# Turning patches with plain identity products, and products that nobody reads in TensorE's waits

## The reference, cut to what matters

```python
x  # (4, 3, 224, 224)
patches = x.reshape(b, c, hp, P, wp, P)              # P = 8, so 28 x 28 patches of 8 x 8 x 3 = 192 features
patches = jnp.transpose(patches, (0, 2, 4, 3, 5, 1)).reshape(b, hp * wp, P * P * c)
tokens = layernorm(patches, ln1_g, ln1_b)
tokens = tokens @ W1 + b1                            # 192 -> 64
tokens = layernorm(tokens, ln2_g, ln2_b)
h1 = layernorm(tokens @ Wp1 + bp1, lnp_g, lnp_b)     # the same rows three times over
return jax.nn.silu(h1) @ Wp2 + bp2
```

## Time and profile before

| what | value |
|---|---|
| median of the timed runs | 605.25 us (603.64 to 606.86) |
| span of the profiled execution | 604.2 us |
| TensorE busy | 561.1 us, 93% of the span |
| VectorE busy | 376.7 us, 62% |
| ScalarE busy | 337.7 us, 56% |
| chain that ended last, TensorE's share | 90% |

### The profile page before, as it was taken

One profiled execution on the slowest core, in us unless ns is written; L12 is line 12 of the kernel. 1 busy time (PEld: TensorE's weight loads), 2 busy tenths in 40 slices (PEclk: granted clock), 3 DMA queues, 4 the chain that ended last, 5 costly groups with the idle time before them and its releaser, 6 DMA issues.

```text
span 604.2 us, 10259 instructions
## 1 busy us (share of the span) xinstructions
PE 561.1 (93%) x3082; PEld 327.0 (54%) x3082; DVE 376.7 (62%) x899; ACT 337.7 (56%) x734; POOL 81.6 (14%) x97
## 2 busy tenths in 40 slices
PE   0699899998999999999999999999999999998993
PEld 0454334443465666666665675675675676544341
DVE  3844654324787676676676676676676677354471
ACT  0464858666674664664564564564564564657331
POOL 0000000000998001001001001001001001120000
PEclk9999799999989999999999999999999999999998
DMA  7500000001623223323223323223323320000015
GB/s 173 230 0 1 1 0 2 0 14 33 157 84 86 73 65 93 79 63 97 72 61 98 73 60 97 75 59 98 76 58 98 76 58 19 2 1 1 1 33 128
DMA packets 21986, 37.65 MB, mean 62 GB/s; under 512 B 5560, under 2 KB 15224, under 8 KB 21704
## 3 DMA queue, kind: packets, MB, share of 16 engines
q1 hardware_dynamic: 21606, 36.82, 23.6%
q10 hardware_dynamic: 354, 0.50, 0.3%
HBM read 6.07 MB, written 2.41 MB: 14 GB/s over the span
## 4 chain that ended last, share of the span: by engine, by line
PE 90%; DVE 3%; ACT 3%; DMA 2%; issue 1%; SPq 0%; DVEq 0%
PE P L775 86%; DMA X<-x 2%; PE P L791 2%; ACT L528 1%; DVE mx L1590 1%; PE P L1089 1%; PE P L1283 1%; DVE bst L1367 1%; SPq L399 0%; ACT PT L655 0%; ACT g L701 0%; PE P L917 0%; DVE xhat L1439 0%; PE P L1072 0%; DVE xn L1380 0%
## 5 line engine op out<-in xcount | busy, mean ns | idle before, releaser
L1590 DVE TENSOR_REDUCE mx<-P 112x1 f32<-112x392 f32 x448 | 218.8, 557 | 93.7 <-PE P L775 89.5
L655 ACT ACTIVATE PT<-P 112x392 f32<-112x392 f32 x448 | 188.5, 495 | 27.3 <-PE P L775 26.0
L775 PE MATMUL P<-Ks,Qs 96*112 96x392 f32 x448 | 166.8, 377 | 0.7 <-ACT XV L623 0.6
L775 PE MATMUL P<-Qs,Ks 98*112 98x392 f32 x448 | 154.0, 349 | 0.8 <-ACT PT L655 0.7
L775 PE MATMUL P<-PT,XVs 112*64 112x392 f32 x896 | 154.7, 496 | 0.0
L775 PEld LDWEIGHTS P<-PT,XVs 112*64 112x64 f32 x896 | 61.4, 137 | 80.0 <-issue 74.2
L775 PEld LDWEIGHTS P<-Ks,Qs 96*112 96x112 f32 x448 | 78.2, 177 | 44.0 <-issue 18.9
L663 ACT ACTIVATE CT<-P 128x392 f32<-128x392 f32 x32 | 15.9, 498 | 128.0 <-PE P L775 128.0
L775 PEld LDWEIGHTS P<-Qs,Ks 98*112 98x112 f32 x448 | 79.1, 178 | 4.8 <-ACT PT L655 2.6
L753 POOL TENSOR_TENSOR OUT<-OUT,part 120x448 f32<-120x448 f32 x27 | 31.1, 1151 | 264.7 <-DVE part L1617 264.7
L775 PE MATMUL P<-VBs,CT 128*112 128x130 f32 (+1 forms) x320 | 40.0, 261 | 0.0
(11 more groups left out here) (197 smaller groups left out, 477.7 us busy)
## 6 DMA issues: line engine op xcount, KB each, us to landing
Qs<-QKH SPq DMA_DIRECT2D x64, 98.0 KB, 2.2
Ks<-QKH SPq DMA_DIRECT2D x64, 98.0 KB, 2.1
XVs<-XV SPq DMA_DIRECT2D x32, 196.0 KB, 2.5
Qs<-QKL SPq DMA_DIRECT2D x32, 98.0 KB, 2.1
Ks<-QKL SPq DMA_DIRECT2D x32, 98.0 KB, 2.1
X<-x SPq DMA_DIRECT2D x4, 588.0 KB
wa<-table_a SPq DMA_DIRECT2D x1, 2207.5 KB, 8.5
VBs<-VB SPq DMA_DIRECT2D x32, 65.0 KB, 2.2
```

Source lines behind the costliest of these rows:

```text
L655: nc.scalar.activation(PT[:, u, c * HALF:(c + 1) * HALF], P[0:T, SCORE_BANK + half_in_loop(s, u, c) % RING, 0:HALF], ACT.Exp, scale=float( ...
L775: return nc.tensor.matmul(dst, lhsT, rhs, start=start, stop=stop, **more)
L1590: nc.vector.tensor_reduce(mx[:, s % 2, c, t:t + 1], bank(n)[0:T, :], AX.X, ALU.max)\
```

## The change

`turn` uses a plain product with the identity (patches as weights, the first 112 columns of the identity as the moving operand) in place of the transpose instruction. A new helper `busy(n, times)` multiplies the identity by the first 389 columns of the table into PSUM bank n; nobody reads that bank before other products overwrite it. It is called in five places of TensorE's stream: three products as soon as the pixels are in and ahead of turn(0); two after project(6); one in the first norm's `weights(2)`; one each in the second norm's `folded(1)` and `folded(2)`; two after the second norm's spread, ahead of the products with wp2c.

```diff
@@ -788,9 +788,13 @@
                 pe.wait_ge(xn_ready, g + 1)
                 for q in range(4):
                     for k in range(2):
-                        last = nc.tensor.transpose(P[0:KF, 2 * p + k, q * T:(q + 1) * T], xn[:, p, q, k * KF:(k + 1) * KF],
-                                                   A("ident", T)[:, 0:T])
+                        last = mm(P[0:KF, 2 * p + k, q * T:(q + 1) * T], xn[:, p, q, k * KF:(k + 1) * KF], A("ident", T)[:, 0:T])
                 last.then_inc(turned, 1)
+
+            def busy(n, times):
+
+                for _ in range(times):
+                    mm(P[:, n, 0:EARLY_A], A("ident"), wa[:, 0:EARLY_A])
 
             def project(g, p):
                 pe.wait_ge(xT_ready, 2 * g + 2)
@@ -800,6 +804,8 @@
                                   k == 0, k == 1)
                 last.then_inc(patch_full, 1)
 
+            pe.wait_ge(pixels_in, 16 * B)
+            busy(6, 3)
             turn(0, 0)
             pe.wait_ge(w1_ready, 1)
 
@@ -810,6 +816,7 @@
                 project(2 * i + 1, 1)
             repeat(pe, 0, 3, {}, two)
             project(6, 0)
+            busy(6, 2)
 
 
             def norm(S, source=None, count=None, meanwhile=None):
@@ -847,12 +854,15 @@
                 elif b == 2:
                     pe.wait_ge(bias_in, 1)
                     mm(P[:, 0, 0:1], wp1c[:, :], col("ln2_b")).then_inc(bias_full, 1)
+                    busy(6, 1)
 
             def folded(b):
                 if b == 0:
                     for h in range(2):
                         last = mm(P[h * D:(h + 1) * D, 5, 0:HEADS * D], A("fold", D), A("vo", D))
                     last.then_inc(vo_full, 1)
+                elif b < B - 1:
+                    busy(7, 1)
 
             pe.wait_ge(means_set, 1)
             norm(TOK2, meanwhile=weights)
@@ -862,6 +872,7 @@
                 mm(bank(b), wp1g[:, :], xhat[:, b, :]).then_inc(main_full, 1)
             pe.wait_ge(woy_ready, 1)
             norm(POOL3, meanwhile=folded)
+            busy(7, 2)
             for b in range(B):
                 pe.wait_ge(silu_ready, b + 1)
                 mm(bank(b), wp2c[:, :], act[:, b, :]).then_inc(centred, 1)
```

## The result

The changed kernel took 596.45 us (median of four executions, 596.15 to 598.7) beside 605.49 us for the kernel before (603.64 to 606.86); the ratio is 0.986 with an interval of 0.984 to 0.989. The profiled execution has a span of 594.3 us and a time of its own of 596.15, so 1.85 us lie outside the span. A span and the time of the same execution are thus two things, also for the kernel before, where the span of 604.2 was taken as the time.

What follows compares the result with a forecast made beforehand. TensorE at half clock was taken to bound the patch stage; gains of 2.4 (patches), 1.8 (first norm), 2.65 (wp1g) and 0.75 (second norm) sum to 7.6, span 604.2 to 596.6, plus 1.05 gives 597.6 us, range 595 to 600.

Steps and rivals of the forecast that it cites:

- the likeliest case: Whole kernel: the forecast of 597.6 us holds, with its own range of 595 to 600; chance 0.72.
- the largest term: Patch stage: TensorE at full clock shortens the groups, put at -2.4 us after a 0.3 charge.
- The turn at full clock: Patch stage: 16 plain-product instructions take 1.67 us at full clock, as long as the transposes were.
- the projection: Patch stage: each group's projection on TensorE goes from 1.69 to about 0.95 us at full clock.
- The third rival: Patch turns: a plain product costs four transposes, so a turn takes 2.99 us, the kernel 605.1; chance 0.02.
- The group: Patch stage: one turn-and-projection group goes from 3.35 to 2.8 us, five groups gaining 2.7.
- the loop over ScalarE and VectorE: Patch stage: turn, ScalarE, VectorE, then next-but-one turn take 5.65 us per two groups, setting 2.8 a group.
- the 0.3 I charged for a late rise: Patch stage: 0.3 us taken off the gain because the clock rises only between 19.4 and 21.9 us.
- First norm: First norm: variances -0.65, `weights` no longer delaying the spread -0.4, spread -0.75; -1.8 us together.
- wp1g to the second norm's spread: Products with wp1g to the second norm's variances: 7.09 us becomes 4.4 at full clock, a gain of 2.65.
- the second spread: Second norm: the spread at full clock gains 0.75 us, its fillers fitting into existing waits.
- the first rival: Clock lost again where no filler is, likeliest the third norm; 601.0 us (600 to 603.5), chance 0.14.

Runs made afterwards that it cites:

- the bridged run: Changed kernel with the original single transposes back, all fillers kept and two more fillers after turn(0); 597.13 us, ratio 0.987 to the kernel before.

## Why the prediction was right

The direction, the size and the mechanism in the norms were right; 596.45 lies in the narrower range given for the likeliest case, 1.15 below the forecast. The reason given for the clock in the patches was wrong, and the largest term was put too low. By its steps:

The turn at full clock was put at 1.67 and took 1.77 with its modelled end (1.70 to the next projection); the projection at 0.95 is 0.96 (23.97 to 24.93). The third rival, four transposes for a product, is out: 16 instructions took 1.77, eight transposes 0.97.

The group was put at 2.8, limited by the loop over ScalarE and VectorE, with gaps on TensorE ahead of the turns; from 22.26 to 35.70 it is 13.44 / 5 = 2.69, the lower end given. The loop did not bind: VectorE's reciprocal comes at 28.92, when ScalarE's sd has been there since 28.60. VectorE's own work sets the pace, as in the bridged run, where its turns start 2.67 apart after 0.79 of idling on TensorE. And what the prediction did not see, TensorE has no slack either: 1.70 and 0.97 are 2.67, and from 27.75 to 37.49 it has no gap. This is the term that was mis-sized most: the patches gained 3.49 and not 2.4, of which the groups are 0.6. The rest of that difference is the 0.3 I charged for a late rise, which came before turn(0), and a tail of 3.5 in place of 3.70 after the last turn. The early rise is luck of the execution: the filler ahead took 3.73 here and 4.26 in most of the other profiles that have it, and there turn(0) or more was still in part at half clock. (The 0.66 for one of its instructions should have read 5.57 / 8 = 0.70, or 4.2 for six.)

First norm 1.8, measured 1.87; wp1g to the second norm's spread 2.65, measured 2.70; the second spread 0.75, measured 0.64. The fillers delayed neither spread by more than hundredths: ScalarE's exponentials ended at 45.52 and 54.11, the fillers ahead of the spreads at 45.55 and 54.15, and the spreads began at 45.58 and 54.16; so there is no room for one more. The wp2c products were said to buy nothing and gave 0.23. The clock in the third norm, the first rival, was not lost: TensorE's wait there was 0.81. Together the steps are 8.9 against 7.6 by 72 us; the measured difference of medians is 9.04.

That the forecast was off by 1.15 only is in part luck. The spans differ by 9.9, that is 2.3 more than the 7.6: 1.3 in the steps, 0.26 from the pixels and 0.7 from the fall of the clock at 175 us. I carried 1.05 us from span to median, where the profiled execution of the changed kernel has 1.85 between its span and its own time and a median 0.3 above that: 1.1 of the 2.3 was taken back.

What was wrong is the reason given for the clock in the patches. I read 21.7 us of work without a gap at half clock as the transposes' doing, and cited the Trainium skill for it (TensorE: Matmul & The Clock Gate, Part 4). The sum did not hang on that, only on the clock being up with the new turns; but the reason was refuted by transposes that held the clock (596.61), raised it (0.98 at 24.61) and raised it amid projections (603.93 beside 604.12), and by single ones that held it (0.97 at 30.76). Measurement and page differ here, for float32 transposes, and the measurement decides. What the plain product brings is that it is twice the work: sixteen transposes in its place give the same time.

## What to carry to other kernels

Read TensorE's clock from durations of the same instruction in two stages, not from the granted share alone, which says full ahead of its first change. Where a stage runs at half clock, put work that nobody reads into the long waits ahead of it and inside it; it is free as long as it ends before the wait does. Either half of this change alone gave less than two thirds of the whole (602.23 and 600.06 against 596.45), since in both the clock had come up and was lost again at a wait that was left open (2.29 and 1.71 us). Before you change the instruction that seems to keep the clock down, fill the waits around it: here the old transposes, with two more fillers, had the fastest execution but one of all (595.13), if two slower ones beside it.

## What the runs showed of the hardware that was not expected

A float32 transpose on TensorE follows the clock as a product does (sixteen in 1.67 from one start to the next at full, eight in 1.66 at half), and the clock is raised and held with it as with plain products. A float32 product with the identity costs as much as two of them (1.77 against 1.74 for sixteen instructions).

The clock fell after waits of 1.51 us (in the kernel before), 1.71 and 2.29 us, and stayed up in waits of 0.79 to 1.04 us. But the last wait alone does not decide it. In the run of plain products alone the clock stayed up through a wait of 1.51 and fell with the next one, of 1.56. And in the kernel before it fell once where no wait from 160 us on had been longer than 0.63 (the granted clock reads 1.00 up to 175.0, 0.60 in the half us behind it, then 0.50):

```profile
173.47 0.43 PE L775 MATMUL P<-Ks,Qs 96*112 96x392 f32 x1 [0.63 <-ACT XV L623]
173.74 0.34 PE L775 MATMUL P<-Qs,Ks 98*112 98x392 f32 x1
...
176.28 0.53 PE L775 MATMUL P<-Qs,Ks 98*112 98x392 f32 x1
```

The changed kernel has the same waits there and kept the clock. What decides was not shown; a wait that cost nothing in one execution can cost the clock in the next.

When the clock rises differs between executions, as the first turns show, and so do falls in late stages: the granted clock falls between 165 and 185 us in five of the fourteen profiles, and in the last mixture of experts, between 545 and 553 us, in three others. The times scatter along with the mean clock: four executions of the changed kernel with a mean clock of 0.995, 0.995, 0.991 and 0.985 took 596.15, 596.48, 596.42 and 598.70 us.
